# Row biases written into the sums' PSUM banks by ScalarE, GpSimd left with the norms' roots, and new cyclic orders on all five engines

## What is computed

```python
h = gelu(x @ Wi[e] + bi[e]);  o = h @ Wo[e] + bo[e]
x = norm(o + x) * gamma[e] + beta[e]
```

```python
out = gelu(x @ w1 + b1) @ w2 + b2                                # c = 0 or 1
out = gelu(gelu(x @ w1 + b1) @ w2 + b2) @ w3 + b3                 # c = 2
x = norm(x + out) * gamma2 + beta2
```

```python
x = norm(x) * (1 + scale_t) + shift_t
q, k, v = x @ Wq + bq, x @ Wk + bk, x @ Wv + bv
x = x + softmax(q k^T / 4 + bias[b, h] + mask) v @ Wo + bo
x = x + gelu2(norm(x) * g2 + beta2) @ W1 ... @ W2 + b2
```

## Time and profile before

| | |
|---|---|
| median of 3 runs | 2161.42 us (2157.35 to 2162.31) |
| the profiled execution | 2160.82 us, its span 2159.0 us, granted clock 0.975 |
| TensorE matmul / weight load busy | 1946.9 us (90%) / 1688.8 us (78%) |
| VectorE busy | 1610.5 us (75%) |
| ScalarE busy | 1363.3 us (63%), 438.8 us of it 342 table loads |
| GpSimd busy | 293.6 us (14%) |
| DMA queue | 352.99 MB, 52.6% of 16 engines |

### The profile page before, as it was taken

The page is one execution under the profiler, slowest core; times in us unless marked ns, Lnnn a source line. Parts: engine busy times, 40 slices in busy tenths (PEclk is TensorE's granted clock), DMA queues, the critical chain, the costliest instruction groups (busy, mean ns, idle before and its releaser), DMA issues.

```text
span 2159.0 us, 43618 instructions
## 1 busy us (share of the span) xinstructions
PE 1946.9 (90%) x14354; PEld 1688.8 (78%) x14354; DVE 1610.5 (75%) x5373; ACT 1363.3 (63%) x2179; POOL 293.6 (14%) x393
## 2 busy tenths in 40 slices
PE   5678999999999999999999999999999999999876
PEld 4567888888888888888788787888888887888665
DVE  4357778888777788877777887777888877777753
ACT  3246667676666776677677666666676676677332
POOL 1111101111110111111111111111111111111100
PEclk8689999999999999999999999999999999999888
DMA  6364556555455566554556555556555555654430
GB/s 217 111 185 147 160 156 195 182 191 183 152 166 149 176 193 188 167 174 130 184 178 187 178 160 177 150 186 197 181 188 182 168 150 155 193 179 137 134 104 10
DMA packets 222312, 356.13 MB, mean 165 GB/s; under 512 B 29523, under 2 KB 120147, under 8 KB 222068
## 3 DMA queue, kind: packets, MB, share of 16 engines
q1 hardware_dynamic: 222068, 352.99, 52.6%
HBM read 294.12 MB, written 58.79 MB: 163 GB/s over the span
## 4 chain that ended last, share of the span: by engine, by line
PE 69%; DVE 19%; issue 6%; ACT 3%; DMA 1%; SPq 0%; POOL 0%; ACTq 0%; DVEq 0%; POOLq 0%
PE pD L441 45%; PE pX L656 11%; PE pS L441 9%; DVE bias_ring L1142 8%; DVE bias_ring L939 6%; PE pC L441 2%; PE pC L678 1%; DVE x_nat L936 1%; DVE crossed L936 1%; ACT gelu_out L746 1%; ACT L746 1%; DMA branch_row<-in_branch_rows 1%; ACT probs L746 1%; ACT hid L746 0%; DVE ctx_nat L936 0%
## 5 line engine op out<-in xcount | busy, mean ns | idle before, releaser
L1142 DVE CUSTOM_DVE_ANT_0 bias_ring<-pS,bias_ring 128x256 f32<-128x256 f32 x1024 | 389.7, 418 | 226.9 <-PE pS L441 225.1
L746 ACT ACTIVATE probs<-pX 128x512 f32<-128x512 f32 x512 | 304.4, 595 | 235.7 <-PE pX L656 233.8
L746 ACT ACT_TABLE_LOAD x342 | 438.8, 1283 | 22.3 <-PE pD L441 15.6
L656 PE MATMUL pX<-ident,bias_ring 128*128 128x128 f32 x2048 | 325.4, 282 | 115.9 <-DVE bias_ring L939 97.3
L656 PEld LDWEIGHTS pX<-ident,bias_ring 128*128 128x128 f32 x2048 | 227.8, 141 | 218.5 <-DVE bias_ring L939 209.9
L939 DVE TENSOR_SCALAR bias_ring<-bias_ring,row_max 128x256 f32<-128x256 f32 x1024 | 338.4, 373 | 18.3
L441 PE MATMUL pS<-k_stack,q_stack 96*128 96x256 f32 x1024 | 304.7, 380 | 0.0
L441 PE MATMUL pD<-x,raw 128*128 128x256 f32 x1024 | 251.4, 389 | 5.1 <-ACT gelu_out L746 2.6
L441 PE MATMUL pD<-raw,gelu_out 128*128 128x256 f32 x1024 | 237.6, 380 | 2.8 <-DVE y_nat L936 2.8
L441 PEld LDWEIGHTS pD<-x,raw 128*128 128x128 f32 x1024 | 191.4, 194 | 31.2 <-issue 7.5
L441 PEld LDWEIGHTS pS<-k_stack,q_stack 96*128 96x128 f32 x1024 | 197.9, 193 | 20.1 <-issue 0.2
(11 more groups left out here) (148 smaller groups left out, 3679.4 us busy)
## 6 DMA issues: line engine op xcount, KB each, us to landing
bias_ring<-in_fside SPq DMA_DIRECT2D x512, 256.0 KB, 3.3
raw<-in_experts SPq DMA_DIRECT2D x128, 512.0 KB, 4.6
q_spill<-hid SPq DMA_DIRECT2D x96, 256.0 KB, 3.5
k_spill<-hid SPq DMA_DIRECT2D x96, 256.0 KB, 3.4
q_stack<-q_spill SPq DMA_DIRECT2D x128, 192.0 KB, 3.5
k_stack<-k_spill SPq DMA_DIRECT2D x64, 384.0 KB, 4.8
norm<-in_expert_rows SPq DMA_DIRECT2D x32, 384.0 KB, 4.0
x_nat<-in_x SPq DMA_DIRECT2D x32, 256.0 KB, 3.1
```

What stands on the lines that cost most here:

```text
L656: last = e.transpose(pX[:, k, t * P:(t + 1) * P], bias_ring[:, u % NBIAS, t, k * P:(k + 1) * P], ident[:, :])
L746: return e.activation(o, i, func, bias=bias, scale=scale)
L1142: e.tensor_tensor_reduce(bias_ring[:, n, t, :], pS[:, t, :], bias_ring[:, n, t, :], 1.0, -3.4e38, ALU.add, ALU.max, row_max[:, n, t:t + 1] ...
```

## The change

1. TensorE opens banks `SUM_F` and `SUM_T` once in the setup, with one matmul each. After that no product opens them: `wide_out`, `branch_out`, `Wo` and `narrowed` all run with start=False.
2. ScalarE gets four new steps for each batch, `row_seed`: a copy of a broadcast row (128x512) into the bank, before the first product that adds to it. One stands in wide after gelu 1 (`expert_seeded`), one in front after the first branch step (`branch_seeded`), two in tail, before and after the second high half (`o_seeded`, `ff_seeded`). TensorE's `wide_out(0)`, `branch_out`, `Wo` and `narrowed(0)` wait for them.
3. GpSimd's four `biased` are gone, and with them four waits of VectorE (one of them is replaced by a wait for `y1_turned`).
4. `load_branch_row(b + 1)` is issued right after the spill of k, two steps earlier in SyncE's queue, and waits for `branch_seeded`.
5. `ORDER` and `SKIP` of all engines are new. ScalarE's converting of the weights in the setup starts one step later.

```diff
 ORDER = {
-    "PE": "hhfhhfhhhhfrrhhfrhhfhhhghhhghhrhhghhhhhhgrgrhhgghhrgghhrfhhhhfrrhhfr",
-    "ACT": "rhrhrfhrrhfrrrhfrhfrfhhfhrfrhfhhrhghhghhhgrhghg",
-    "DVE": "hrhfrhrfhrhfhhrfhrfhghrhhhrhhfhfrhrhrfhrfghrfg",
-    "POOL": "ffrgrfgf",
-    "SP": "hfhfhhfhhhhffggrhhhhhhghghg",
+    "PE": "frhhfhhrfhhhrhhhfrhhfrhhfrhhfhfhhhrgrghhrghhrhhhghhhgghhghhghhhhhhgr",
+    "ACT": "hhrrhfhfhrrfrhhrrhfrrhffrrhffhfrhhrgrrgrhhgghhhghhg",
+    "DVE": "hfrhhrrhfhrfhfgrfhhrrhrhrhhhfhhfhfhhgrfrhrfhrg",
+    "POOL": "ffrg",
+    "SP": "hhfhhhhghhhrffhhhhhgghghffg",
 }
-SKIP = {"PE": (9, 101, 37), "ACT": (13, 56, 55), "DVE": (12, 53, 47), "POOL": (4, 0, 6), "SP": (10, 42, 4)}
+SKIP = {"PE": (12, 113, 43), "ACT": (14, 60, 64), "DVE": (11, 54, 48), "POOL": (2, 0, 3), "SP": (8, 45, 4)}
...
+            for bank in (SUM_F, SUM_T):
+                last = mm(pD[:, bank, :, :], ident[:, 0:1].to_broadcast([P, P]), ident[:, 0:1].unsqueeze(2).to_broadcast([P, 2, H]), True, True)
+            last.then_inc(sem["sums_opened"], 1)
...
-                    if m2 == 0 and b:
-                        e.wait_ge(sem["dve_sum2"], T * b)
+                    if m2 == 0:
+                        e.wait_ge(sem["expert_seeded"], b + 1)
...
+            def row_seed(bank, row):
+
+                return act(pD[:, bank, :, :], row.unsqueeze(1).to_broadcast([P, T, H]), ACT.Copy)
...
+                    if m2 == 1:
+                        if b:
+                            e.wait_ge(sem["dve_sum2"], T * b)
+                        else:
+                            e.wait_ge(sem["sums_opened"], 1)
+                        e.wait_ge(sem["dma_norm1"], 16 * (b + 1))
+                        row_seed(SUM_F, norm1[:, 2, :]).then_inc(sem["expert_seeded"], 1)
+                        yield
...
+                e.wait_ge(sem["dve_sum1"], T * (b + 1))
+                e.wait_ge(sem["dma_brow"], 16 * (b + 1))
+                row_seed(SUM_F, branch_row[:, :]).then_inc(sem["branch_seeded"], 1)
+                yield
...
+                row_seed(SUM_T, o_row[:, :]).then_inc(sem["o_seeded"], 1)
+                yield
                 e.wait_ge(sem["ffn_turned"], b + 1)
                 act(flat(xc_hi[:, :, :]), flat(pD[:, TAIL, :, :]), ACT.Copy).then_inc(sem["x3_hi"], 1)
+                yield
+                e.wait_ge(sem["dve_xo"], T * (b + 1))
...
+                row_seed(SUM_T, ff_row[:, :]).then_inc(sem["ff_seeded"], 1)
                 yield
...
-            def biased(rows, bias, name):
-                e.tensor_tensor(rows[:, :, :], rows[:, :, :], bias.unsqueeze(1).to_broadcast([P, T, H]), ALU.add).then_inc(sem[name], 1)
```

More of the change, by code:

```diff
@@ L57 @@
     "dma_stack1", *(f"dma_bias{n}" for n in range(7)),
[3 rows of a table removed]
+    "dve_wide", "dve_front", "dve_sum1", "dve_sum2", "x0_made", "x0_turned", "x0_copied", "wide_in", "wide_gelu", "wide_out",
+    "y1_scaled", "y1_made", "y1_turned", "x1_hi", "x1_lo", "pe_narrow", "act_narrow", "dve_narrow", "pe_deep", "act_deep",
+    "dve_deep", "branch_done", "sums_opened", "expert_seeded", "branch_seeded", "x2_made", "x2_turned", "x2_hi", "x2_lo", "qkv", "qk_hi", "qk_lo",
     "v_made", "mask_made",
     "scored", "max_made", "subtracted", "turned", "exp_made", "valued", "ctx_copied", "ctx_turned", "rden_made", "ctx_made",
-    "dve_tail", "dve_xo", "ctxT", "ctx_hi", "ctx_lo", "wo", "ffn_in_made", "ffn_turned", "x3_biased", "x3_hi", "x3_lo",
+    "dve_tail", "dve_xo", "ctxT", "ctx_hi", "ctx_lo", "wo", "ffn_in_made", "ffn_turned", "o_seeded", "ff_seeded", "x3_hi", "x3_lo",
     "hid_seeded", "w1", "tanh", "gated", "ffn_hi", "ffn_lo", "w2", "out_made",
@@ L305, in load_branch_row @@
                 if b:
-                    e.wait_ge(sem["y1_biased"], b)
+                    e.wait_ge(sem["branch_seeded"], b)
                 c = e.value_load(idx[0:1, 1, b:b + 1], min_val=0, max_val=2)
@@ L400, in front @@
                     load(to[:, 2 - 2 * i, :, :], both[:, 0, :, :], "dma_spill")
+                    if i and b + 1 < NB:
+                        load_branch_row(b + 1)
                     yield
@@ L587, in branch_out @@
                     ins = [(hid[:, 0, 0, n, :], hid[:, 0, 1, n, :]) for n in range(2)]
+                    e.wait_ge(sem["branch_seeded"], b + 1)
                     c = e.value_load(idx[0:1, 1, b:b + 1])
@@ L710, in tail @@
                 yield
-                if b:
-                    e.wait_ge(sem["out_made"], b)
+                e.wait_ge(sem["o_seeded"], b + 1)
                 xc_parts = [(xc_hi[:, k, :], xc_lo[:, k, :]) for k in range(K)]
                 e.wait_ge(sem["ctx_hi"], b + 1)
-                to_natural(SUM_T, "Wo", 0, xc_parts, (sem["ctx_lo"], b + 1)).then_inc(sem["wo"], 1)
+                to_natural(SUM_T, "Wo", 0, xc_parts, (sem["ctx_lo"], b + 1), start=False).then_inc(sem["wo"], 1)
                 yield
@@ L727, in narrowed @@
                     n = 4 * b + m2
+                    if m2 == 0:
+                        e.wait_ge(sem["ff_seeded"], b + 1)
                     e.wait_ge(sem["ffn_hi"], n + 1)
                     ins = [(ffn[:, n % 2, 0, i, :], ffn[:, n % 2, 1, i, :]) for i in range(2)]
-                    to_natural(SUM_T, "W2", 2 * m2, ins, (sem["ffn_lo"], n + 1), m2 == 0).then_inc(sem["w2"], 1)
+                    to_natural(SUM_T, "W2", 2 * m2, ins, (sem["ffn_lo"], n + 1), start=False).then_inc(sem["w2"], 1)
                 hidden(0)
@@ L759, in piece @@
                         act(w_hi[:, a0:a1], staged(i, a0, a1), ACT.Copy, scale=scale).then_inc(sem["act_w"], 1)
-                for pieces in ((), (), (), (0,), (1,), (2, 3), (4,), (5,), (6,), (7,), (8,), (9,), (10,)):
+                for pieces in ((), (), (), (), (0,), (1,), (2, 3), (4,), (5,), (6,), (7,), (8,), (9,), (10,)):
                     for i in pieces:
@@ L882, in tail @@
                 yield
+                if b:
+                    e.wait_ge(sem["out_made"], b)
+                else:
+                    e.wait_ge(sem["dve_folded"], 1)
+                row_seed(SUM_T, o_row[:, :]).then_inc(sem["o_seeded"], 1)
+                yield
                 e.wait_ge(sem["ffn_turned"], b + 1)
                 act(flat(xc_hi[:, :, :]), flat(pD[:, TAIL, :, :]), ACT.Copy).then_inc(sem["x3_hi"], 1)
+                yield
+                e.wait_ge(sem["dve_xo"], T * (b + 1))
+                if not b:
+                    e.wait_ge(sem["dma_bcast"], 64)
+                row_seed(SUM_T, ff_row[:, :]).then_inc(sem["ff_seeded"], 1)
                 yield
@@ L1245, in front @@
             def front(b):
-                e.wait_ge(sem["y1_turned"], b + 1)
-                e.wait_ge(sem["dma_brow"], 16 * (b + 1))
-                biased(y_nat, branch_row[:, :], "y1_biased")
-                yield
                 for i in range(2):
@@ L1264, in tail @@
                 root("tail", b, 1e-5)
-                yield
-                e.wait_ge(sem["ffn_in_made"], b + 1)
-                e.wait_ge(sem["dma_bcast"], 64)
-                biased(res[:, b % 3, :, :], ff_row[:, :], "x3_biased")
                 yield
```

23 lines of the change are left out of this document (5 added, 18 removed), and 3 rows, old and new, of the table SEMAPHORES.

## The result

The changed kernel takes **2201.9 us** (median of 4 runs, 2200.0 to 2211.0) where the kernel before takes 2161.0 (2157.4 to 2162.3) beside it: a ratio of 1.020, 95% interval 1.0169 to 1.0231. The forecast was 2148, within 2110 to 2182. It is slower by 41 us, and outside the range.

A forecast was written before the change was run, and what follows sets the result against it. TensorE, busy for 90% of the span, sets the pace, so only its idle time can be won. 19 x (-1.0) + 9 x 0.3 + 5 - 1 - 1 = -13 us against 2160.8 gives 2148 us, range 2110 to 2182.

The forecast's parts named there:

- The order of TensorE: Work between scores and turn, against 1.69 us needed: waits of 4.7 become 3.7, a narrow cycle 1.0 us shorter.
- `scaled` burst: VectorE's second such burst, placed at head 5, was to make TensorE wait 0.4 us.
- restarts and the branch instructions: The 1.6 us of TensorE's idle in a narrow cycle not put to waits; it was to stay.
- The deep batch's 2.1 us: TensorE's wait ahead of branch_out in deep batches, where only values cover the 3.09 us after branch_middle.
- Narrow and deep cycles: Batch cycles without and with the deep branch: 60.4 us, 1.0 shorter, and 66.3 us, 0.3 longer.
- Wo's wait for o_row: In the tail, ScalarE's high half and then seed expose TensorE's product Wo to a 0.9 us wait.
- Fill and drain: First three rounds +5 us at wide_out 0 and -1; last three cycles -1.
- The reloads: ScalarE's reloads around gelu: five groups in a narrow cycle, six in a deep one, 342 before and after.
- More is won: Rival: VectorE catches up in the waits added one by one, 2109 or 2116 us; chance 0.20.
- 0.7 us a cycle: Idle before turns caused by GpSimd's adds lengthening VectorE's subtraction; 0.7 us of each cycle was to go.
- ScalarE turns into the chain: Rival: between turns 11 and 13 ScalarE comes late and one reload a cycle shows, 2184 us; chance 0.23.
- The stalls only move: Rival: VectorE's and ScalarE's bursts find other heads, the old idle of 6.4 us returns, 2161; chance 0.15.

The follow-up runs named there:

- e1: The changed kernel with the load of norm3 issued two steps earlier in SyncE's queue; 2156.8 us, 0.997 of the kernel before.
- e6: e1 with TensorE's branch_out one place later, behind heads 9 and 10, and VectorE's branch sum behind the maxima of head 10; 2148.2 us.
- e7: e6 with ScalarE's write of o_row moved ahead of its copy of ctx; 2146.5 us, 0.994 of the kernel before.
- e13: The kernel before with the new orders, GpSimd's adds kept, the branch's row at its new place and norm3 loaded early; 2165.5 us.
- e8: The kernel before with only norm3's load moved later, behind the bias of head 7 of the next batch; 2283.7 us, 1.058.
- e11: e1 with the deep branch's code left out on all engines, the choice between two narrow branches kept (another model's output); 2083.0 us, 0.966.

## Why the prediction was wrong

- **The step that failed** is a part that wasn't costed at all, in "The order of TensorE": VectorE's scaling that makes x2 has no term there, neither for its length nor for what it waits for. The `scaled` burst that the text puts at head 5, with 0.4 us, is another one, the expert's, as the trace after has it between the maxima of heads 4 and 5 (the row below). The text follows the branch's row in SyncE's queue ("issued ten us ahead of its seed") and costs it at nothing, rightly. It doesn't follow norm3 in the same queue, which stays behind the stacks while its reader moves ahead by three heads. Before, it was issued 19 us ahead of its use, so no row of the waits named it. In the changed kernel it was issued 4.6 us ahead of the time at which VectorE could have used it (5.9 less the wait of 1.3), and takes 5.9. That cost 45 us (e1), of the 54 between forecast and result: 1.3 us a cycle by the wait, and 0.5 by the clock. The forecast took TensorE at full clock through the whole middle.

```profile
1309.61 0.87 DVE L976 SCALAR_TENSOR_TENSOR y_nat<-x_nat,wide_mean_var,norm 128x256 f32<-128x256 f32 x2
```

- **Two more misses.** The 1.6 us of "restarts and the branch instructions" were taken over unchanged, as if "issue" were a constant. TensorE now stops in some cycles where code behind a jump lands: 8.5 us in e1. That it is because branch_in, branch_middle and branch_out stand closer together is likely, but not shown; with branch_out one place later (e6, e7) stops stayed. And each wait was priced at its own length. The deep batch's 2.1 us was forecast rightly (1.94), but in four of nine deep cycles the clock fell behind it, 1.5 us more each; with the stops that is 11.9 us in e1. In sum the middle of the changed kernel's profiled execution is 73.8 us longer than forecast: 36.9 for norm3, 25.6 for the clock, 11.3 left for stops and what follows them.
- **Narrow and deep cycles** were forecast at 60.4 and 66.3; e1 shows 60.5 and 66.3. Wo's wait for o_row of 0.9 us (0.80 in the trace), the deep wait ahead of branch_out of 2.1 us (2.0), the subtraction at 352 ns (351), POOL at 121 us (121.6) and the normalising at 408 ns (407) came as written. These terms of the forecast were right, for an undisturbed cycle of a kernel whose norm3 is early. Its gain of 16 us in the middle was not reached even there: the 28 cycles of e1 take 1764.7 us, 20.4 more than forecast and 4.7 more than before.
- **Fill and drain** were given +3 us; with 392.9 against 400.8 they gained 7.9. Here the forecast was too careful by 11 us, and in e1 this hides over half of what the middle has too much: 2156.9 = 1764.7 + 392.2, against the forecast's 1744.3 + 403.8. That e1 comes within 9 us of 2148 is luck to that extent. The clock takes 55.9 us in the ramps of the kernel before, 49.1 in the changed one's and 45.7 in e1's, so the clock alone may have made the gain, and no run separates it from the order.
- **The reloads** were forecast at 342; there are 336, worth 7.7 us of ScalarE, off the path.
- **The rivals.** "More is won" is not seen. That GpSimd's adds lengthen VectorE's pieces, by which it would have been 2109, is real in the rows (379 to 351 ns). But e1 is 10 us faster than e13, not 52, and the profiled executions have none of it in the middle. The forecast's own 0.7 us a cycle for it isn't seen there either. "ScalarE turns into the chain" gave a time near the result, 2184, but by another mechanism. No exponential of heads 11 to 13 makes TensorE wait, and the reloads stay hidden. "The stalls only move" is nearest in kind: with norm3 early, the middle is within 5 us of what it was, and with norm3 late the stall that came was one which the old order had kept out of sight.

What stays open: why norm3's landing went from 4.0 to 5.9 us. In the old order norm3 was the last of six loads, with none behind it for 8.3 us; in the new one five bias loads follow it at once, and bias loads went from 3.3 to 6.2 at the median. e8 shows 6.4 amid a burst in the old order, e1 4.5 at its earlier place in the new one. Whether the loads just ahead of it or those just behind it make it slow wasn't separated by a run of its own.

## What to carry to other kernels

When an order is changed, list for each moved step every load that it waits for, and work out issue, landing and use anew for each. A load that appears in no wait of the old profile isn't free, it is early, and its lead can be spent by moving its reader. In a kernel whose main engine is 90% busy, one load of 256 KB that comes 1.3 us late in each batch costs 2%, more than the change around it was worth. And price a stop of TensorE of about 2 us at more than its length, since the clock can fall behind it: here two short waits, 1.4 us together, saved more against one of 1.9 than the half microsecond between them.

## What the runs showed of the hardware

- The granted clock went from full to half behind stops of TensorE of about 2 us (1.94 behind `hid`; 1.57 and 0.80 with two transposes between them), but not behind each. Fallen clocks in the middle: before 0, after 14, e1 7, e6 1, e7 0, e8 13 (more than one stretch long in 7 of them), each costing 1.7 us of work at full clock or a multiple of it.
- TensorE stopped for 1 to 4.3 us near the branch, in the middle of a row of products or ahead of branch_out, with no wait in the trace, where a packet of 16 KB of instructions landed behind conditionals that skip 24 products. In e11, with jumps over 12 products only and less code, there was no such stop in 28 cycles. The longest in the changed kernel was 4.3 us, by its weight loads. The kernel before has such conditionals and no stop like these in its middle.
- A load of the same 256 KB took 4.0, 4.5, 5.9 or 6.4 us from issue to landing at the median (before, e1, after, e8). Between before and e8, and between e1 and after, nothing but its place among the other loads differs.
- ScalarE's write of a row into a bank that was opened once, with accumulation on it from then on, took 584 to 602 ns in the mean, by the row, as its other writes of 128x512 do (598 for the hidden bias before).
